# First group's bias by a small product and a copy through DRAM, small bias products ahead of the conditioning, one idle product fewer

## What is computed

```python
h = jax.nn.gelu(embedding @ W0 + b0, approximate=False)
h = jax.nn.gelu(h @ W1 + b1, approximate=False)
att = jax.nn.softmax((h @ W2 + b2) / T, axis=-1)
agg_w = jnp.einsum('bk,koi->boi', att, weight[..., 0])
agg_b = att @ bias_k
out = jnp.einsum('boi,bih->boh', agg_w, x) + agg_b[:, :, None]
```

## Time and profile before

| | |
|---|---|
| median of 3 runs | 543.12 us |
| lowest, highest | 542.98, 543.97 us |
| profiled execution, its own time | 544.38 us |
| its span | 542.6 us |
| PE busy | 530.3 us, 98% |
| DVE busy | 244.2 us, 45% |
| ACT busy | 140.9 us, 26% |
| POOL busy | 157.3 us, 29% |

### The profile page before, as it was taken

How to read it: one execution, slowest core, us unless ns; L and a number is a source line. 1 busy time by engine, 2 the same in 40 slices (tenths; PEclk the granted TensorE clock), 3 DMA queues, 4 the chain that set the end, 5 groups by cost and what they waited for, 6 DMA issues and landing times.

```text
span 542.6 us, 6969 instructions
## 1 busy us (share of the span) xinstructions
PE 530.3 (98%) x2647; PEld 394.1 (73%) x2647; DVE 244.2 (45%) x537; ACT 140.9 (26%) x247; POOL 157.3 (29%) x153
## 2 busy tenths in 40 slices
PE   7999999999999999999999999999999999989996
PEld 6888888888888888888888886635455445577774
DVE  3543322722223723233622434453525258897775
ACT  5422222322222322222322222000002217545232
POOL 3599992300000400000300920040002000127666
PEclk9999999999999999999999999999999999999999
DMA  9398440197000230000305000969695819589763
GB/s 308 108 423 301 160 102 0 41 160 127 0 0 0 77 97 0 0 0 0 88 11 137 0 1 0 154 137 171 182 216 155 220 49 211 105 155 211 179 137 117
DMA packets 82502, 61.60 MB, mean 114 GB/s; under 512 B 61744, under 2 KB 66864, under 8 KB 81712
## 3 DMA queue, kind: packets, MB, share of 16 engines
q1 hardware_dynamic: 77696, 41.83, 35.4%
q0 software_dynamic: 4704, 19.40, 14.2%
q10 hardware_dynamic: 80, 0.08, 0.0%
HBM read 38.98 MB, written 12.81 MB: 95 GB/s over the span
## 4 chain that ended last, share of the span: by engine, by line
PE 92%; DVE 4%; issue 1%; ACT 1%; DMA 1%; POOL 0%; DVEq 0%; POOLq 0%
PE ps L659 90%; DVE xs L1180 1%; PE ps L858 1%; DVE cT L1180 1%; DMA pack_a<-in_pack_a 1%; DVE c_lo L1180 0%; DVE cT L1354 0%; DVE c_lo_odd L1180 0%; PE ps L819 0%; DVE t L1180 0%; PE ps L975 0%; PE ps L872 0%; ACT c_hi_odd L1054 0%; ACT c_hi L1054 0%; ACT wT L1054 0%
## 5 line engine op out<-in xcount | busy, mean ns | idle before, releaser
L659 PE MATMUL ps<-c_hi,wl 128*128 128x512 f32 x448 | 169.9, 389 | 0.0
L659 PE MATMUL ps<-c_lo,wl 128*128 128x512 f32 x448 | 169.7, 389 | 0.0
L1180 DVE TENSOR_TENSOR hff<-silu,ps 128x512 f32<-128x512 f32 x56 | 38.5, 688 | 161.2 <-PE ps L659 158.5
L659 PEld LDWEIGHTS ps<-c_lo,wl 128*128 128x128 f32 x448 | 84.1, 188 | 17.5
L659 PEld LDWEIGHTS ps<-c_hi,wl 128*128 128x128 f32 x448 | 84.0, 188 | 17.5
L659 PE MATMUL ps<-wl,h_hi 128*128 128x512 f32 x224 | 87.7, 391 | 0.0
L659 PE MATMUL ps<-wl,h_lo 128*128 128x512 f32 x224 | 87.2, 389 | 0.0
L1088 ACT ACTIVATE silu<-ps 128x512 f32<-128x512 f32 x56 | 33.5, 598 | 119.8 <-PE ps L659 119.6
L1180 DVE TENSOR_TENSOR h_lo<-hff,h_hi 128x512 fp32r<-128x512 f32 x56 | 46.5, 830 | 39.1 <-ACT h_hi L1054 39.1
L1054 ACT ACTIVATE h_hi<-hff 128x512 fp32r<-128x512 f32 x56 | 35.4, 632 | 107.4 <-DVE hff L1180 107.4
L659 PE MATMUL ps<-wbase,cT 128*128 128x512 f32 x128 | 56.5, 594 | 0.0
(11 more groups left out here) (181 smaller groups left out, 582.1 us busy)
## 6 DMA issues: line engine op xcount, KB each, us to landing
wl<-in_wl POOLq DMA_DIRECT2D x14, 768.0 KB, 9.2
stg<-y_dram SPq DMA_DIRECT2D x64, 128.0 KB, 5.2
xs<-in_x SPq DMA_DIRECT2D x4, 1024.0 KB, 8.2
x_all<-in_x SPq DMA_DIRECT2D x1, 4096.0 KB, 15.0
y_dram<-prod SPq DMA_DIRECT2D x16, 256.0 KB, 2.2
x_dram<-x_all SPq DMA_DIRECT2D x4, 1024.0 KB, 6.8
x_all<-cS POOLq DMA_DIRECT2D x4, 1024.0 KB, 7.6
x_all<-in_bias POOLq DMA_DIRECT2D x4, 1024.0 KB, 10.5
```

The lines of the kernel that those rows point to most:

```text
L659: return pe.matmul(o, l, r, start=start, stop=stop)
L1180: return dve.tensor_tensor(o, a, b, op)
```

## The change

Five edits, all in the first 24 us of the program:

1. Four idle products where there were five.
2. The wide bias product is gone, with `terms`, POOL's multiplication and ACT's copy of the bank. In its place PE multiplies attT[:, 0] by kbias into 64x32 of bank 0, ahead of the last two transposes.
3. ACT copies that to btab[:, 0] ahead of the second copy to attT, SP writes the first 16 rows of it (2 KB) to bias0_dram, waits for that, and fetches it with a broadcast to all partitions of bias_bc (256 KB written).
4. The other bias products (layers 2 and 3, layer 1, biasN) move from behind the conditioning to ahead of it on PE. Layer 0's is no longer among them.
5. ACT's later copy of the table leaves out layer 0's column.

```diff
--- before.py
+++ after.py
@@ -168,6 +168,7 @@
         y_dram = nc.dram_tensor("y_dram", (2, NB, ROWS * S, WIN), F32).ap()
         w_dram = nc.dram_tensor("w_dram", (ROWS, S, CB * P), F32).ap()
         x_dram = nc.dram_tensor("x_dram", (NB * ROWS, D), F32).ap()
+        bias0_dram = nc.dram_tensor("bias0_dram", (GB, ROWS), F32).ap()
         bias_dram = nc.dram_tensor("bias_dram", (NB, 4, ROWS), F32).ap()
 
         ps = ctx.enter_context(nc.psum_tensor("ps", [P, 8, 512], F32))
@@ -212,7 +213,6 @@
 
             return xs if g % 2 else cT
 
-        terms = silu[:, 0]
         prod0 = hff[:].rearrange("p b (j k o) -> p (b j) k o", k=K, o=ROWS)
 
 
@@ -240,7 +240,8 @@
         s_att_bc = sem("s_att_bc")
         s_att_turned = sem("s_att_turned")
         s_attT = sem("s_attT")
-        s_terms = sem("s_terms")
+        s_btab0 = sem("s_btab0")
+        s_bias0_dram = sem("s_bias0_dram")
         s_bias0 = sem("s_bias0")
         s_mix0 = sem("s_mix0")
         s_blk_half = sem("s_blk_half")
@@ -415,6 +416,10 @@
                     src = x_dram[(g * GT + j) * P:(g * GT + j + 1) * P].rearrange("(b i) n -> i b n", b=TB)
                     sp.dma_start(xT(g)[j * ROWS:(j + 1) * ROWS], src).then_inc(s_xT[g], 16)
 
+            sp.wait_ge(s_btab0, 1)
+            sp.dma_start(bias0_dram, btab[0:GB, 0]).then_inc(s_bias0_dram, 16)
+            sp.wait_ge(s_bias0_dram, 16)
+            sp.dma_start(bias_bc[:], bias0_dram.rearrange("b o -> (b o)").unsqueeze(0).broadcast_to([P, GB * ROWS])).then_inc(s_bias_bc[0], 16)
             sp.wait_ge(s_btab, 2)
             sp.dma_start(bias_dram, btab[:]).then_inc(s_bias_dram, 16)
             sp.wait_ge(s_bias_dram, 16)
@@ -552,10 +557,6 @@
             weights(0, 3)
 
             pool.wait_ge(s_pack_c, 16)
-            pool.wait_ge(s_attT, 1)
-            pool.tensor_tensor(terms.rearrange("p (b o) -> p b o", o=ROWS),
-                               attT[:, 0, 0:GB].unsqueeze(2).broadcast_to([P, GB, ROWS]),
-                               kbias[:, 0:ROWS].unsqueeze(1).broadcast_to([P, GB, ROWS]), ALU.mult).then_inc(s_terms, 1)
             split_c(0)
             weights(3, M)
             pool.wait_ge(s_att_bc, 2)
@@ -675,7 +676,7 @@
 
 
             pe.wait_ge(s_set, 2)
-            for n in range(5):
+            for n in range(4):
                 mm(bank(7)[:, 0:P], ones[:], ones[:])
             pe.wait_ge(s_att, 7)
             mm(bank(3)[:, 0:NT * K], selrep, att_m[:, 0]).then_inc(s_att_spread, 1)
@@ -684,12 +685,11 @@
             pe.wait_ge(s_att, 9)
             mm(bank(2)[:, 0:NT * K], strip2[:].rearrange("b c o -> b (c o)"), att_m[:, 1])
             mm(bank(2)[:, NT * K:2 * NT * K], selrep, att_m[:, 2]).then_inc(s_att_spread, 1)
+            pe.wait_ge(s_attT, 1)
+            mm(bank(0)[0:NB, P:P + ROWS], attT[:, 0], kbias[:, 0:ROWS]).then_inc(s_bias0, 1)
             for i in (1, 2):
                 ins = pe.transpose(bank(1)[:, (i - 1) * NB:i * NB], att_m[:, i], ident[0:NB, 0:NB])
             ins.then_inc(s_att_turned, 1)
-
-            pe.wait_ge(s_terms, 1)
-            mm(bank(0), ones[:], terms).then_inc(s_bias0, 1)
 
             def nothing():
                 pass
@@ -779,6 +779,15 @@
                 down(g, M - 1)
 
 
+            pe.wait_ge(s_attT, 2)
+            for l, i in COND.items():
+                if l > 0:
+                    mm(bank(1)[0:NB, l * ROWS:(l + 1) * ROWS], attT[:, i], kbias[:, i * ROWS:(i + 1) * ROWS])
+            mm(bank(1)[0:NB, ROWS:2 * ROWS], condT, cwT)
+            for b in range(TB):
+                ins = mm(bank(1)[b * ROWS:(b + 1) * ROWS, P:P + NT], kbias[:, COND[2] * ROWS:(COND[2] + 1) * ROWS],
+                         attT[:, COND[2]].rearrange("p (t b) -> p b t", b=TB)[:, b])
+            ins.then_inc(s_bias_mm, 1)
             pe.wait_ge(s_staged[0], 16)
             for ready, js in ((s_blk_half, (0, 1)), (s_blk[0], (2, 3))):
                 pe.wait_ge(ready, 1)
@@ -788,14 +797,6 @@
                     if 3 in js:
                         ins.then_inc(s_cond_mm[0], 1)
 
-            pe.wait_ge(s_attT, 2)
-            for l, i in COND.items():
-                mm(bank(1)[0:NB, l * ROWS:(l + 1) * ROWS], attT[:, i], kbias[:, i * ROWS:(i + 1) * ROWS])
-            mm(bank(1)[0:NB, ROWS:2 * ROWS], condT, cwT)
-            for b in range(TB):
-                ins = mm(bank(1)[b * ROWS:(b + 1) * ROWS, P:P + NT], kbias[:, COND[2] * ROWS:(COND[2] + 1) * ROWS],
-                         attT[:, COND[2]].rearrange("p (t b) -> p b t", b=TB)[:, b])
-            ins.then_inc(s_bias_mm, 1)
             with pe.Fori(0, G - 1) as g:
                 layer0(g, True)
             layer0(G - 1, False)
@@ -1066,11 +1067,11 @@
             act.activation(att[:], att[:], ACT.Exp).then_inc(s_aexp, 1)
             act.wait_ge(s_att_turned, 1)
             copy(attT[:, 0], bank(0)[:, 0:NB]).then_inc(s_attT, 1)
+            act.wait_ge(s_bias0, 1)
+            copy(btab[:, 0], bank(0)[0:NB, P:P + ROWS]).then_inc(s_btab0, 1)
             act.wait_ge(s_att_turned, 2)
             copy(attT[:, 1:3].rearrange("p i n -> p (i n)"), bank(1)[:, 0:2 * NB]).then_inc(s_attT, 1)
             act.activation(scrap[:], scrap[:], ACT.Silu)
-            act.wait_ge(s_bias0, 1)
-            copy(bias_bc[:], bank(0)).then_inc(s_bias_bc[0], 16)
             copy(att_bc[:, 1:3].rearrange("p i n -> p (i n)"), bank(2)[:, 0:2 * NT * K]).then_inc(s_att_bc, 1)
             act.wait_ge(s_mix0, 3)
             copy(att_bc[:, 0], bank(3)[:, 0:NT * K]).then_inc(s_att_bc, 1)
@@ -1093,7 +1094,7 @@
 
             split_c(0)
             act.wait_ge(s_bias_mm, 1)
-            copy(btab[:].rearrange("b l o -> b (l o)"), bank(1)[0:NB, 0:4 * ROWS]).then_inc(s_btab, 1)
+            copy(btab[:, 1:4].rearrange("b l o -> b (l o)"), bank(1)[0:NB, ROWS:4 * ROWS]).then_inc(s_btab, 1)
             copy(biasN, bank(1)[:, P:P + NT]).then_inc(s_biasN, 1)
             with act.Fori(0, G - 1) as g:
                 layer0(g, True)
```

## The result

The changed kernel takes 545.97 us (median of 13 runs, 545.1 to 547.68) where the kernel before takes 543.79 (13 runs, 542.62 to 544.38). The medians differ by 2.18 us, 0.40%. The ratio over all runs is 1.0049 with a 95% interval of 1.0041 to 1.0057, 2.7 us, which is the difference of the means (546.34 and 543.65). The forecast was 543.0, 0.1 us under the 543.12 that the kernel before had in its first three runs: no change.

What follows compares the result with a forecast made beforehand. PE, busy 98% of the span, was taken as the bound. Terms -0.05 - 0.18 + 0 = -0.23 us, with +0.1 for the bias, gave 544.38 - 0.13, or 543.0 us against the median; range 542.2 to 544.5.

Steps and rivals of the forecast that it cites:

- the bias through DRAM: Layer 0's bias by write (3.5 us) and broadcast (2.4 us): ready at 17.9 us, wanted about 18.2, so costed at nothing.
- the bias that stands on the edge: Allowance of +0.1 us in the sum, for the bias landing just before DVE wants it.
- the second rival: Bias lands after 18.2 us, delaying cT, c_hi, c_lo and second slice in full; 19.8 gives +1.5 us; chance 0.10.
- wrong altogether: Sign that the whole prediction fails: the second slice of layer 0 starts before 23 us or after 25.
- the one for the late bias: Sign in the profile: DVE's cT waits on the DMA to bias_bc.
- The small products: Seven small bias products ahead of the conditioning take 1.4 us from 12.5; conditioning starts at 13.9, a gain of 0.05.
- The first rival: TensorE's clock steps up later in the conditioning, perhaps at 18.3 to 19.6 us: +0.9 us, time 543.9; chance 0.27.
- What goes from behind the conditioning: Small products leaving there free 0.77 us on PE; second slice starts at 23.83 instead of 24.01, gain 0.18 us.
- The idle product: One idle product less before the spreading of att_m brings that forward by 0.28 us, at most 0.34.
- 1.05 + 1.87 us off the chain: Apparent saving on the chain of waits, POOL's terms plus PE from wide product to conditioning: 2.9 us in all.

## Why the prediction was wrong

Kernels by their difference to the runs of before beside them:

| kernel | us | conditioning: start, length in the profile | the clock's step in that profile |
|---|---|---|---|
| before | 0 | 13.95, 5.58 | 17.8 |
| four idle products | -0.37 | 13.58, 4.82 | 15.9 |
| three idle products | +0.07 | 13.45, 4.39 | 14.7 |
| four idle, three wide ones in front of the conditioning | +0.84 | 14.71, 4.43 | 16.2 |
| four idle, small products in front of it | +1.33 | 14.87, 5.35 | 18.0 |
| bias through DRAM alone | +1.72 | 12.85, 5.80 | 17.0 |
| the same, slices held | -0.02 | 12.90, 6.15 | 17.7 |
| the same, slices held, four idle | -0.39 | 12.72, 6.19 | 17.8 |
| the change | +2.18 | 13.24, 6.09 | 18.1 |
| the change, second profile | | 13.28, 5.17 | 16.2 |
| the change, third slice held | +0.37 | 13.64, 6.38 | 18.9 |
| the change, both slices held | +0.24 | 13.37, 6.22 | 18.4 |

The step is the first record of the conditioning whose successor starts 0.11 us behind it and not 0.21.

*The step that failed is the bias through DRAM,* the term costed at nothing and then at 0.1 us "for the bias that stands on the edge". I took 3.5 us for the write and 2.4 for the broadcast. They took 5.12 and 3.08 (4.52 and 3.08 in the second profile; the broadcast 3.0 to 3.3 in every other kernel), so the bias stood at 19.9 us (19.4 in the second) instead of 17.9, 1.6 us past 18.3. The row that I had in hand said it: the table's copy under load took 5.8 us. I had set the landing at 15.4 us, when the engines had drained after the heavy traffic up to 14 us. The idea was right, since the write lands just behind the last weight slice, but I took the drain from the DMA share and not from that slice's landing. In the kernel before it landed at 7.2 + 8.6 = 15.8 us, as this view of wl shows:

```profile
L491 POOL DMA_DIRECT2D wl<-in_wl x3: 558/577/740, 6.0 to 7.2; - x3
DMA to landing us min/median/max: 6.1/7.3/8.6
```

In the two profiles of the changed kernel it landed later still, at 16.7 and 16.1 us. Of the 2.0 us by which the bias was later than forecast in the first profile, 1.4 are the write's landing (16.8 for 15.4) and 0.7 the broadcast. The held slices show the cause: 1.3 and 2.2 us for the same write, and 1.9 and 1.8 us of the loss gone. The mechanism was the second rival, "the bias comes late", with a chance of 0.10 that was much too small. It had said that every us counts in full, since nothing can go in between. That held up to the second slice: with the bias through DRAM alone, cT came 1.45 us later than before and the second slice 1.40; in the second profile of the change, 1.08 and 1.04. Choosing the end near the only row under load would have put the case above the forecast. The sign for "wrong altogether", the second slice after 25 us, came in both profiles (26.72 and 25.05), and so did the one for the late bias, cT waiting on the DMA.

The rival's own price was still too low: it had +1.5 us for a bias at 19.8. One reason can be the deadline. The 18.3 us were read from the slowest of the 13 executions of before, and with four and three idle products cT started at 17.17 and 16.60. If it starts earlier in a typical execution of before too, the same landing costs more; no second profile of before shows it.

*The clock's fall was not in the sum.* I had thought of a later rise and not that PE would wait for so long as to lose the clock. It is in 5 of 13 runs and costs 1.8 us in each by the two groups' medians, of which 1.1 us can be seen in the profile as products at the lower level. It is not what the 2.2 us are made of: the median run is of the lower group, and that group's own median is 1.9 us over before.

*The small products* took 13.24 - 12.22 = 1.02 us instead of 1.4, and the conditioning started at 13.24 and not at 13.9. So this term was too dear by 0.4 us at its place. But the start 0.7 us earlier gave little: the conditioning took 6.09 us instead of 5.58 and ended 0.2 us earlier. An earlier start alone makes it longer, since more of its records stand before the clock's step: 22 of 32 here, 18 before. The step itself came 0.3 us later than in the profile of before, and 1.6 us earlier in the second execution. So two executions of one kernel lie 1.9 us apart, nearly half as far as all kernels of the table, and the profiles do not show that the change puts the step off. The rival had counted the step from the end of PE's last gap, 5.7 us in the profile of before; in the two of the change it came 5.8 and 3.9 us behind it. The first rival, "the clock steps up later", had +0.9 us for that; it stays open. It did not decide the changed kernel's two profiles, where the conditioning ended at 19.3 and 18.5 us, ahead of the bias. In the single edits, what the small products cost ahead of the conditioning is 1.7 us without DRAM and 0.6 with it. The forecast took their time as paid by the wide product that goes. With the slices held, the change has both and is 0.6 us slower than four idle products alone (+0.24 against -0.37), so it was not fully paid.

*What goes from behind the conditioning* was right in kind: most of what PE was freed of there came to nothing. With the small products in front and no DRAM, PE is freed of 0.77 us of work behind the conditioning, and the second slice starts 5.62 us after cT, where with four idle products alone it starts 5.71 after it: a gain of 0.09 against 0.18.

*The idle product* was right: 0.28 us forward expected, 0.38 seen in the profile, and 0.37 us of time measured, with an interval that almost reaches no change.

*The bound "1.05 + 1.87 us off the chain"* was rightly distrusted. What was late next was the transfer pair, and by more than I said.

## What to carry to other kernels

A value that goes out to DRAM and back pays for whatever stands in the DMA engines at that moment. Cost such a hop by the landing of the last transfer that was queued ahead of it, and not by the time at which the rate drops. Where the hop must be quick, hold back a prefetch that is not urgent: holding 768 KB of weights that PE first used at 29.5 us (in the kernel before) gave back 1.8 us here. And work taken from TensorE at the beginning of a kernel is not by itself time gained: without the wide product and with the transfers covered, the conditioning started 0.9 us earlier and the kernel took the same time. Before one profile is compared with another, a second execution of the same kernel shows how much of a difference is the execution's own: here the clock's step moved by 1.9 us.

## What the runs showed that was not expected

- A 2 KB write took 5.1, 4.6, 4.7 and 4.5 us behind three weight slices, 2.2 behind two and 1.3 behind one. Behind two and three it landed 0.2 us after the last slice, so it is that slice's landing that decides.
- TensorE's granted clock fell to 0.50 after a gap of 2.02 us and stayed at 1.00 through one of 2.35 us in another execution of the same kernel. The length of the gap alone does not decide, and the same code falls into two groups of times 1.8 us apart.
- The broadcast of 2 KB pieces took 3.0 to 3.3 us with no other traffic, where the 256 KB stores in long pieces had a median of 2.4. That all its reads go to the same 2 KB did not make it faster than a store.
- Taking away one of five products that compute nothing made the kernel 0.37 us faster, because the fifth stood in front of a product whose input was ready. With four or three of them the profiles showed no later clock: its step came at 15.9 and 14.7 us, where it came at 17.8 before. With three the time was that of before again (+0.07), and why is open.
